# Gathering rows from a four-group loop with a ring of sixteen index columns, in a graph-network kernel

## The chip, the cores and the metric

One Trainium2 chip, one of its cores. The metric is the device time of one execution in microseconds (us), median of several runs. TensorE (PE) multiplies, VectorE (DVE), ScalarE (ACT) and GpSimd (POOL) work on tiles in on-chip memory, SyncE (SP) issues plain transfers. Only GpSimd issues indirect transfers here, the gathers of this case.

## The reference, cut to what matters

Four layers of message passing over one graph with 6250 nodes and 100000 edges, sorted by destination, features of 128 float32. Each layer reads a row of a node table for the source of every edge, combines it with something of the edge and of its destination, and reduces over the edges of one destination:

```
h1   = relu([x[src], edge_attr] @ W1a + b1a) @ W1b + b1b; segment_sum(h1, dst)     # layer 1
m    = xl[src] + xr[dst] + e_attr @ We;  logits = (leaky(m) * att).sum             # layer 2, twice
h3   = relu([x[dst], x[src] - x[dst]] @ W1 + b1) @ W2 + b2; segment_max(h3, dst)   # layer 3, three times
```

These are the six places where rows are gathered by `src`. Layer 0 (an attention layer) needs no such gather: it makes its rows by products and scatters sums instead.

## The kernel before

Edges are laid out in steps of 128, none of which crosses a block of 128 destinations. Four steps make a group (`GROUP = 4`), and every stage runs over 208 groups (`GROUPS`), the loops in trips of four groups (`RING = 4`, `trips = 52`), so that the buffer number `r = n % 4` is fixed in the code of a trip. `srci` holds the source numbers of all steps in on-chip memory, one column of 128 int32 for each step. One indirect transfer reads one column and brings 128 rows of the table from memory into a part of buffer `R[r]`, so a group takes four of them; each has a semaphore of its own, `rows_in[r][u]`.

The order between engines is kept by counting semaphores. A `Signal` starts with a lead of four, so `wait_ge(s, s.done(n - RING))` waits until group n-4 has been done, and lets the first four groups through.

**GpSimd before.** In `edge_mlp_sums` (line 987, layer 1), `edge_logits` (line 1198, twice in layer 2) and `edge_maxima` (line 1674, three times in layer 3) GpSimd's code has no loop: all 208 groups (209 in `edge_maxima`) are written out, each with a wait for its buffer and four transfers that name their column of `srci` directly. In `edge_mlp_sums` and `edge_maxima` the wait is part of the first of the four transfers. In `edge_logits` there are two waits: one on `products_made`, with a step `sem_inc(pool_gate)` of its own, and one on `rows_free_again`, which is part of the first transfer.

**What frees a buffer.** In `edge_mlp_sums` it is `rows_added`: DVE has added the gathered rows to PE's products (`join`, line 1058). In `edge_logits` it is `products_made` (PE, lines 1247 and 1249) and `rows_free_again`, which SP counts up (line 1210) once it has also stored the gathered rows to memory. In `edge_maxima` it is `edges_made`: PE has turned the rows (line 1713) and added the destinations' part (line 1717).

**The round of `edge_maxima`.** For every group PE runs `make_products(n)` (line 1723; waits for ACT's relu of group n), `make_edges(n + 1)` (1713, 1717), `turn(n - 1)` (1705) and `make_ends(n - 3)` (1730). ACT runs `lay(n + 2)` (1755), `relu(n + 1)` (1761; waits for `edges_made` of group n+1) and `turn_out(n - 1)` (1766). DVE runs the running maximum `scan(n)` (1802), `make_hots`, `add` (964) and `mark_ends`.

**ACT.** It does one relu per group in `edge_mlp_sums` (line 1043) and nothing in `edge_logits`.

**A stage that scatters.** `add_messages` in layer 0 is not changed, but it already has the form of the new code: GpSimd loops over 52 trips, waits at steps of its own (`sem_inc(pool_gate)`) and names columns of `slots`, a tile of sixteen columns, that DVE writes (line 835) before each group's four scatters (line 882).

Of the kernel before, what the change touches and what calls it, by code (L numbers as in the profile page):

```python
# [25 lines left out]
P = 128  # L26
# [94 lines left out]
def build(nc, I, out):  # L121
    ctx = ExitStack()
    with ctx:
# [843 lines left out]

        def edge_mlp_sums():
# [11 lines left out]
            with nc.Block() as block:  # L980
                @block.gpsimd
                def _(gp):
                    for n in range(GROUPS):
                        gp.wait_ge(rows_added.h, rows_added.done(n - RING))
                        for u in range(GROUP):
                            k = LEAD + n * GROUP + u
                            gp.indirect_dma_start(part(R[n % RING], u), None, gather_d[:, :],  # L987
                                                  bass.IndirectOffsetOnAxis(ap=srci[:, k:k + 1], axis=0)).then_inc(rows_in[n % RING][u].h, 16)
# [47 lines left out]
                @block.scalar  # L1036
                def _(act):
                    relued.lead(act)
                    with act.Fori(0, trips) as j:
                        for r in range(RING):  # L1040
                            n = j * RING + r
                            act.wait_ge(rows_added.h, rows_added.done(n))
                            S_.activation(M[r], M[r], ACT.Relu).then_inc(relued.h, 1)

                @block.vector
                def _(dve):
# [45 lines left out]
                    add(GROUPS - 1, RING - 1, ends)  # L1092
            for s in (edges_made, sums_made, relued, rows_added, hots_made, added):
                s.passed(GROUPS + RING)
# [80 lines left out]
        def edge_logits(heads, width, table, att, we):  # L1175
# [13 lines left out]
            with nc.Block() as block:  # L1189
                @block.gpsimd  # L1190
                def _(gp):
                    for n in range(GROUPS):
                        gp.wait_ge(products_made.h, products_made.done(n - RING))
                        gp.sem_inc(pool_gate.h, 1)
                        gp.wait_ge(rows_free_again.h, rows_free_again.done(n - RING))
                        for u in range(GROUP):
                            k = step_of(n) + u
                            gp.indirect_dma_start(part(R[n % RING], u, width), None, table[:, :],  # L1198
                                                  bass.IndirectOffsetOnAxis(ap=srci[:, k:k + 1], axis=0)).then_inc(rows_in[n % RING][u].h, 16)
# [53 lines left out]
                def _(dve):  # L1253
# [28 lines left out]
                    for r in range(RING):  # L1282
# [3 lines left out]
                        reduce(n, r)  # L1286
            for s in (products_made, logits_in, logits_made, rows_free_again):
                s.passed(GROUPS + RING)
# [5 lines left out]
            pool_gate.passed(GROUPS)  # L1294
# [360 lines left out]
        def edge_maxima(w2, next_weights):  # L1655
# [11 lines left out]
            with nc.Block() as block:  # L1667
                @block.gpsimd
                def _(gp):
                    for n in range(GROUPS + 1):  # L1670
                        gp.wait_ge(edges_made.h, edges_made.done(n - RING))
                        for u in range(GROUP):
                            k = LEAD + n * GROUP + u
                            gp.indirect_dma_start(part(R[n % RING], u), None, gather_d[:, :],  # L1674
                                                  bass.IndirectOffsetOnAxis(ap=srci[:, k:k + 1], axis=0)).then_inc(rows_in[n % RING][u].h, 16)
# [71 lines left out]
                def _(act):  # L1747
                    for s in (relued, laid):
                        s.lead(act)
                    turned_out.lead(act, 1)  # L1750

# [6 lines left out]
                    def relu(n, i):  # L1758
                        act.wait_ge(edges_made.h, edges_made.done(n))
                        act.wait_ge(products_made.h, products_made.done(n - 2))  # L1760
# [10 lines left out]
                    relu(0, 0)  # L1771
                    with act.Fori(0, trips) as j:
                        for r in range(RING):
# [4 lines left out]
                            relu(n + 1, 1 - r % 2)  # L1778
# [4 lines left out]
                def _(dve):  # L1783
# [53 lines left out]
                    add(GROUPS - 1, 1, ends[2 * GROUP:])  # L1837
            loaded.passed(16 * len(next_weights))
# [113 lines left out]
```

## Time and profile before

| | us |
|---|---|
| median of 3 runs | 11882.29 |
| lowest, highest | 11880.79, 11889.4 |
| span of the profiled execution | 11983.4 |
| GpSimd busy in that span | 6587.1 |
| PE / DVE / ACT busy | 7468.0 / 6860.6 / 2573.8 |
| mean granted TensorE clock | 0.773 |

The profiled execution is one execution under the profiler; its span is from the first to the last instruction, and no other time of that execution is given. Busy times of engines overlap. A stage's start and end are read from the first and last gather of its line: about 2273 to 3560 us (`edge_mlp_sums`), 3820 to 5095 and 6042 to 7325 (`edge_logits`), and three stretches between 8014 and 11940 (`edge_maxima`).

### The profile page before, as it was taken

How to read it: one execution, taken by the hardware profiler on the slowest of the kernel's cores; microseconds unless marked ns; L12 is line 12 of the kernel's file. 1: busy time of each engine (PE TensorE's matmuls, PEld its weight loads, DVE VectorE, ACT ScalarE, POOL GpSimd, SP SyncE). 2: the span in 40 equal slices, each digit the busy share in tenths (PEclk: the TensorE clock that was granted, in tenths of full speed). 3: DMA queues.
4: the chain of work that ended last, by engine and by line, in shares of the span. 5: the costliest groups of instructions: out<-in, count | busy, mean ns of one | idle time of the engine just before them, and what ended most of it. 6: DMA issues, size and time to landing. Idle time of an engine off the chain costs nothing. (4 is left out here: it accounts for less than half of the span.)

```text
span 11983.4 us, 181872 instructions
## 1 busy us (share of the span) xinstructions
PE 7468.0 (62%) x39289; PEld 6257.1 (52%) x39290; DVE 6860.6 (57%) x13795; ACT 2573.8 (21%) x9089; POOL 6587.1 (55%) x6703
## 2 busy tenths in 40 slices
PE   5944444366665777736565554667777676766676
PEld 4944444355555555524454444655555555555555
DVE  6845444433335888866644445665555555565555
ACT  3500000111111000036600001333333233323332
POOL 0088888466651666613256663326666566646665
PEclk8956666555557888879976666779999899989998
DMA  4355555322223666645444443423333333333333
GB/s 124 73 96 96 96 95 95 98 66 66 67 58 76 216 215 213 219 85 160 128 119 127 127 128 100 113 79 130 129 131 130 118 131 129 129 117 130 131 131 120
DMA packets 829515, 1435.73 MB, mean 120 GB/s; under 512 B 184832, under 2 KB 495468, under 8 KB 788960
## 3 DMA queue, kind: packets, MB, share of 16 engines
q1 hardware_dynamic: 532336, 981.36, 25.8%
q0 software_dynamic: 297072, 453.23, 17.4%
q14 instruction: 75, 0.61, 0.0%
q8 instruction: 32, 0.52, 0.0%
HBM read 1114.85 MB, written 320.07 MB: 120 GB/s over the span
## 5 line engine op out<-in xcount | busy, mean ns | idle before, releaser
L1674 POOL DMA_INDIRECT T<-gather_d,srci x2508 | 2386.0, 951 | 1655.8 <-remote 618.6
L1723 PE MATMUL PS<-T,W 128*128 128x512 f32 x1248 | 816.5, 741 | 1102.5 <-issue 601.4
L882 POOL DMA_INDIRECT added_d<-T,slots x832 | 1293.7, 1555 | 284.0 <-issue 215.6
L1249 PE MATMUL PS<-T,ident 128*128 128x256 f32 (+1 forms) x3328 | 1086.0, 410 | 544.6 <-issue 377.1
L964 DVE TENSOR_TENSOR T<-T,PS 128x128 f32 (+1 forms) x2098 | 561.0, 286 | 1267.7 <-remote 935.2
L1247 PE MATMUL PS<-T 128*128 x3328 | 1050.4, 400 | 347.5 <-issue 343.7
L1198 POOL DMA_INDIRECT T<-wide_d,srci x832 | 844.2, 1015 | 686.0 <-PEq L71 267.6
L987 POOL DMA_INDIRECT T<-gather_d,srci x832 | 822.2, 988 | 583.9 <-issue 232.9
L1249 PEld LDWEIGHTS PS<-T,ident 128*128 128x128 f32 x3328 | 717.7, 244 | 768.7 <-issue 463.9
L1198 POOL DMA_INDIRECT T<-gather_d,srci x832 | 800.4, 962 | 578.8 <-issue 234.5
L1469 PE MATMUL PS<-T 128*128 128x260 f32 (+1 forms) x3328 | 758.5, 384 | 445.8 <-DVEq L1522 392.7
L1263 DVE SCALAR_TENSOR_TENSOR T<-W,ew,PS 128x256 f32<-128x256 f32 (+1 forms) x1664 | 575.3, 408 | 775.6 <-remote 757.6
L1247 PEld LDWEIGHTS PS<-T 128*128 128x128 f32 x3328 | 733.5, 246 | 460.0 <-issue 403.3
L1448 POOL TENSOR_TENSOR T<-T,LG 128x256 f32<-128x256 f32 (+1 forms) x840 | 420.6, 522 | 1001.2 <-PE PS L1469 740.3
L1802 DVE TENSOR_TENSOR_SCAN T<-T,PS 128x512 f32<-128x512 f32 x624 | 796.2, 1276 | 243.6 <-issue 214.1
L1761 ACT ACTIVATE T<-PS 128x512 f32<-128x512 f32 x627 | 374.3, 597 | 2517.1 <-remote 1830.0
L1469 PEld LDWEIGHTS PS<-T 128*128 128x128 f32 x3328 | 594.7, 228 | 609.7 <-DVEq L1522 521.0
L800 PE MATMUL PS<-T 128*128 128x128 f32 x1664 | 421.1, 433 | 779.4 <-DVE T L839 779.4
L1723 PEld LDWEIGHTS PS<-T,W 128*128 128x128 f32 x1248 | 200.9, 202 | 1217.4 <-issue 887.4
L800 PEld LDWEIGHTS PS<-T 128*128 128x128 f32 x1664 | 360.3, 319 | 836.5 <-DVE T L839 836.5
L1717 PE MATMUL PS<-T 128*128 128x128 f32 x5016 | 760.4, 302 | 45.8 <-DVE T L1808 44.0
L1518 DVE TENSOR_TENSOR T<-T,PS 128x260 f32 (+1 forms) x1664 | 562.7, 354 | 381.6 <-issue 212.1
(254 smaller groups left out, 15227.1 us busy)
## 6 DMA issues: line engine op xcount, KB each, us to landing
T<-quads_d SPq DMA_DIRECT2D x315, 1024.0 KB
T<-edge_rows_d SPq DMA_DIRECT2D x210, 512.0 KB
edge_rows_d<-T SPq DMA_DIRECT2D x209, 512.0 KB
T<-onehot_t_d SPq DMA_DIRECT2D x416, 256.0 KB
T<-gather_d,srci POOLq DMA_INDIRECT x4172
T<-edge_rows_d SPq DMA_DIRECT2D x210, 256.0 KB
onehot_t_d<-T SPq DMA_DIRECT2D x208, 256.0 KB
edge_rows_d<-T SPq DMA_DIRECT2D x208, 256.0 KB
```

What stands on the lines that cost most here:

```text
L800: last = T_.matmul(part(bank(2 + i), u), part(EQ[i], u), part(MS[i], u), start=True, stop=True)
L882: gp.indirect_dma_start(added_d[u][:, :], bass.IndirectOffsetOnAxis(ap=slots[:, k:k + 1], axis=0), part(OUT[r], u), None, compute_op=ALU.a ...
L987: gp.indirect_dma_start(part(R[n % RING], u), None, gather_d[:, :], bass.IndirectOffsetOnAxis(ap=srci[:, k:k + 1], axis=0)).then_inc(rows_ ...
L1198: gp.indirect_dma_start(part(R[n % RING], u, width), None, table[:, :], bass.IndirectOffsetOnAxis(ap=srci[:, k:k + 1], axis=0)).then_inc(r ...
L1247: T_.matmul(spot(r, u), part(OT[r], u), T2[:, bass.ds(bs[i * GROUP + u] * width, width)], start=True, stop=False)
L1249: last = T_.matmul(spot(r, u), ident[:, :], part(R[r], u, width), start=False, stop=True)
L1263: last = V.scalar_tensor_tensor(part(M[r], u, width), we, ew[:, bass.ds(step_of(n) + u, 1)], spot(r, u), ALU.mult, ALU.add)
L1469: last = T_.matmul(spot(r, u), part(O[r], u), part(M[r], u, both), start=True, stop=True)
L1674: gp.indirect_dma_start(part(R[n % RING], u), None, gather_d[:, :], bass.IndirectOffsetOnAxis(ap=srci[:, k:k + 1], axis=0)).then_inc(rows_ ...
L1717: last = T_.matmul(part(edges, u), part(AB[r % 2], u), part(OT[r % 2], u), start=False, stop=u == GROUP - 1)
L1723: T_.matmul(bank(2 + i), w2, RT[i], start=True, stop=True).then_inc(products_made.h, 1)
L1802: V.tensor_tensor_scan(SC[i], firsts[r], bank(2 + i), SC[1 - i][:, GROUP * P - 1:GROUP * P], ALU.add, ALU.max).then_inc(scanned.h, 1)
```

## The change

In all six stages GpSimd's code becomes a loop of 52 trips over four groups, and its transfers read their columns from the ring `slots` (sixteen columns, four for each `r`). ACT copies the four columns of a group from `srci` into the ring (`take_numbers`). It copies the first four groups at the start; from then on, when the buffer of group n is free, it copies the columns of group n+4. GpSimd no longer waits for DVE or PE but for ACT's copy (`slots_made`), at a step of its own (`sem_inc(pool_gate)`). In `edge_logits` ACT, idle so far, gets a loop for it, and GpSimd's second wait (`rows_free_again`) is at a step of its own too. In `edge_mlp_sums` and `edge_maxima` the copy stands in front of the relu, behind the same wait.

```diff
+        def take_numbers(n, r):
+            S_.activation(slots[:, r * GROUP:(r + 1) * GROUP], srci[:, bass.ds(LEAD + n * GROUP, GROUP)], ACT.Copy).then_inc(slots_made.h, 1)
+        def gather_group(gp, table, rows, r, width):
+            gp.sem_inc(pool_gate.h, 1)
+            for u in range(GROUP):
+                k = r * GROUP + u
+                gp.indirect_dma_start(part(rows, u, width), None, table[:, :],
+                                      bass.IndirectOffsetOnAxis(ap=slots[:, k:k + 1], axis=0)).then_inc(rows_in[r][u].h, 16)
...
 # edge_mlp_sums, GpSimd
-                    for n in range(GROUPS):
-                        gp.wait_ge(rows_added.h, rows_added.done(n - RING))
-                        for u in range(GROUP):
-                            k = LEAD + n * GROUP + u
-                            gp.indirect_dma_start(part(R[n % RING], u), None, gather_d[:, :],
-                                                  bass.IndirectOffsetOnAxis(ap=srci[:, k:k + 1], axis=0)).then_inc(rows_in[n % RING][u].h, 16)
+                    with gp.Fori(0, trips) as j:
+                        for r in range(RING):
+                            gp.wait_ge(slots_made.h, slots_made.done(j * RING + r))
+                            gather_group(gp, gather_d, R[r], r, P)
 # edge_mlp_sums, ACT
+                    slots_made.lead(act)
+                    for r in range(RING):
+                        take_numbers(r, r)
                             act.wait_ge(rows_added.h, rows_added.done(n))
+                            take_numbers(n + RING, r)
                             S_.activation(M[r], M[r], ACT.Relu).then_inc(relued.h, 1)
...
 # edge_logits, GpSimd and ACT
-                    for n in range(GROUPS):
-                        gp.wait_ge(products_made.h, products_made.done(n - RING))
-                        gp.sem_inc(pool_gate.h, 1)
-                        gp.wait_ge(rows_free_again.h, rows_free_again.done(n - RING))
-                        for u in range(GROUP): ...
+                    with gp.Fori(0, trips) as j:
+                        for r in range(RING):
+                            n = j * RING + r
+                            gp.wait_ge(slots_made.h, slots_made.done(n))
+                            gp.sem_inc(pool_gate.h, 1)
+                            gp.wait_ge(rows_free_again.h, rows_free_again.done(n - RING))
+                            gather_group(gp, table, R[r], r, width)
+                @block.scalar
+                def _(act):
+                    slots_made.lead(act)
+                    for r in range(RING):
+                        take_numbers(r, r)
+                    with act.Fori(0, trips) as j:
+                        for r in range(RING):
+                            n = j * RING + r
+                            act.wait_ge(products_made.h, products_made.done(n))
+                            take_numbers(n + RING, r)
...
 # edge_maxima, GpSimd and ACT
-                    for n in range(GROUPS + 1):
-                        gp.wait_ge(edges_made.h, edges_made.done(n - RING))
-                        for u in range(GROUP): ...
+                    with gp.Fori(0, trips) as j:
+                        for r in range(RING):
+                            gp.wait_ge(slots_made.h, slots_made.done(j * RING + r))
+                            gather_group(gp, gather_d, R[r], r, P)
+                    gp.wait_ge(slots_made.h, slots_made.done(GROUPS))
+                    gather_group(gp, gather_d, R[0], 0, P)
-                    def relu(n, i):
+                    def relu(n, i, r):
                         act.wait_ge(edges_made.h, edges_made.done(n))
+                        take_numbers(n + RING, r)
                         act.wait_ge(products_made.h, products_made.done(n - 2))
                         S_.activation(RT[i], bank(i), ACT.Relu).then_inc(relued.h, 1)
```

## Rows read from the trace of the kernel before

**Rows 1.** Windows: a stage each; busy us and instructions by engine, clock, DMA.

```profile
2273.00:3560.00 1287.00, 837.32 (x3309) 738.33 (x3310) 446.07 (x1235) 131.03 (x207) 822.17 (x832) 0.50 0.24 66
3820.00:5095.00 1275.00, 929.95 (x3328) 700.00 (x3328) 1066.81 (x1446) 0.00 (x0) 844.23 (x832) 0.85 0.66 215
6042.00:7325.00 1283.00, 736.83 (x3328) 629.89 (x3328) 633.24 (x1451) 0.00 (x0) 800.41 (x832) 0.67 0.43 128
8014.00:9290.00 1276.00, 888.11 (x5432) 710.98 (x5432) 707.76 (x1466) 399.64 (x1257) 794.00 (x836) 0.91 0.39 130
```

**Rows 2.** Timeline, GpSimd, edge_maxima: start, duration, line, idle before.

```profile
8309.90 0.94 POOL L1674 DMA_INDIRECT T<-gather_d,srci  x1 [1.35 <-remote]
...
8313.65 0.95 POOL L1674 DMA_INDIRECT T<-gather_d,srci  x1 [0.30 <-issue]
```

**Rows 3.** Timeline, ACT, the same stretch: the relus of two groups.

```profile
8309.75 0.60 ACT L1761 ACTIVATE T<-PS 128x512 f32<-128x512 f32 x1 [3.81 <-remote]
...
8315.79 0.60 ACT L1761 ACTIVATE T<-PS 128x512 f32<-128x512 f32 x1 [4.17 <-remote]
```

**Rows 4.** Timeline, PE, the same stretch.

```profile
8310.40 1.12 PE L1723 MATMUL PS<-T,W 128*128 128x512 f32 x2 [2.18 <-issue]
...
8311.79 1.06 PE L1717 MATMUL PS<-T 128*128 128x128 f32 x8
```

**Rows 5.** Timeline, DVE, the same stretch: the scan.

```profile
8311.87 1.27 DVE L1802 TENSOR_TENSOR_SCAN T<-T,PS 128x512 f32<-128x512 f32 x1
```

**Rows 6.** Timeline, end of the first edge_maxima: GpSimd's last gather.

```profile
9274.51 0.94 POOL L1674 DMA_INDIRECT T<-gather_d,srci  x1 [0.30 <-issue]
```

**Rows 7.** Timeline, ACT, the same end.

```profile
9279.89 0.60 ACT L1761 ACTIVATE T<-PS 128x512 f32<-128x512 f32 x1 [1.34 <-PE PS L1717]
...
9283.41 0.60 ACT L1761 ACTIVATE T<-PS 128x512 f32<-128x512 f32 x1 [0.60 <-PE PS L1717]
```

**Rows 8.** Timeline, DVE and GpSimd, edge_mlp_sums.

```profile
2813.00 0.69 DVE L1058 TENSOR_TENSOR T<-PS,T 128x512 f32<-128x512 f32 x1 [9.64 <-remote]
...
2813.96 1.14 POOL L987 DMA_INDIRECT T<-gather_d,srci  x1 [3.15 <-DVE T L1058]
```

**Rows 9.** Timeline, DVE, add_messages, ahead of the first scatter.

```profile
580.69 0.16 DVE L835 TENSOR_TENSOR slots<-T,LG 128x4 int32<-128x4 f32 x1
```

**Rows 10.** Timeline, ACT and GpSimd, the same stretch.

```profile
580.05 0.60 ACT L863 ACTIVATE T<-PS 128x512 f32<-128x512 f32 x1 [11.55 <-PE PS L800]
```

```profile
581.65 1.80 POOL L882 DMA_INDIRECT added_d<-T,slots  x1 [12.66 <-DVE slots L835]
```

**Rows 11.** Groups by form, ACT: a copy of 128x4.

```profile
L1479 ACT ACTIVATE T<-LG 128x4 f32 x208 | 43.4, 209 | 289.4 <-PE PS L1469 287.4 <-PEq L71 2.0
```

**Rows 12.** Timeline, edge_maxima: eight gathers in one run, and the relu behind.

```profile
8784.75 0.95 POOL L1674 DMA_INDIRECT T<-gather_d,srci  x1 [0.30 <-issue]
```

```profile
8787.34 0.60 ACT L1761 ACTIVATE T<-PS 128x512 f32<-128x512 f32 x1 [3.12 <-remote]
```

**Rows 13.** Window of the slower clock; columns as in rows 1.

```profile
8316.80:8320.10 3.30, 3.30 (x12) 2.27 (x11) 2.48 (x4) 0.86 (x5) 2.39 (x4) 0.50 0.35 124
```

**Rows 14.** Timeline, second edge_logits: first and last gather of sixteen, DVE.

```profile
6601.03 0.94 POOL L1198 DMA_INDIRECT T<-gather_d,srci  x1 [4.80 <-SPq L1210]
...
6619.97 0.94 POOL L1198 DMA_INDIRECT T<-gather_d,srci  x1 [0.30 <-issue]
```

```profile
6624.06 1.12 DVE L1263 SCALAR_TENSOR_TENSOR T<-W,ew,PS 128x128 f32<-128x128 f32 x4 [11.62 <-remote]
```

**Rows 15.** Waits by stage: who, for what, us in total, times, longest.

```profile
POOL T L987 <- DVE T L1058: 224.5, 67, 5.8
```

```profile
POOL T L1198 <- SPq L1210: 160.1, 45, 5.1
```

```profile
POOL T L1198 <- SPq L1210: 212.9, 46, 5.4
```

**Rows 16.** Groups by form, GpSimd: the scatters of add_messages.

```profile
L882 POOL DMA_INDIRECT added_d<-T,slots x832 | 1293.7, 1555 | 284.0 <-issue 215.6 <-DMA added_d<-T,slots 55.8 <-DVE slots L835 12.7
```

More of the change, by code:

```diff
@@ L1092, in _ @@
                     add(GROUPS - 1, RING - 1, ends)
+            slots_made.passed(GROUPS + 2 * RING)
+            pool_gate.passed(GROUPS)
             for s in (edges_made, sums_made, relued, rows_added, hots_made, added):
@@ L1191, in _ @@
                 def _(gp):
-                    for n in range(GROUPS):
-                        gp.wait_ge(products_made.h, products_made.done(n - RING))
-                        gp.sem_inc(pool_gate.h, 1)
-                        gp.wait_ge(rows_free_again.h, rows_free_again.done(n - RING))
[L1196 to L1199, printed above, removed]
+                    with gp.Fori(0, trips) as j:
[15 more added lines that the diff above has]
+                            take_numbers(n + RING, r)
                 @block.sync
@@ L1286, in _ @@
                         reduce(n, r)
+            slots_made.passed(GROUPS + 2 * RING)
             for s in (products_made, logits_in, logits_made, rows_free_again):
@@ L1293, in edge_logits @@
                     rows_in[r][u].passed(16 * trips)
-            pool_gate.passed(GROUPS)
+            pool_gate.passed(2 * GROUPS)
             vv_done.passed(1)
@@ L1669, in _ @@
                 def _(gp):
-                    for n in range(GROUPS + 1):
-                        gp.wait_ge(edges_made.h, edges_made.done(n - RING))
[L1672 to L1675, printed above, removed]
+                    with gp.Fori(0, trips) as j:
[4 more added lines that the diff above has]
+                    gather_group(gp, gather_d, R[0], 0, P)
                 @block.sync
@@ L1750, in _ @@
                     turned_out.lead(act, 1)
+                    slots_made.lead(act)
+                    for r in range(RING):
+                        take_numbers(r, r)
                     def lay(n, i, bs):
@@ L1770, in _ @@
                     lay(1, 1, first[GROUP:])
-                    relu(0, 0)
+                    relu(0, 0, 0)
                     with act.Fori(0, trips) as j:
@@ L1777, in _ @@
                             lay(n + 2, r % 2, bs[r % 2 * GROUP:r % 2 * GROUP + GROUP])
-                            relu(n + 1, 1 - r % 2)
+                            relu(n + 1, 1 - r % 2, (r + 1) % RING)
                             turn_out(n - 1, 1 - r % 2)
@@ L1837, in _ @@
                     add(GROUPS - 1, 1, ends[2 * GROUP:])
+            slots_made.passed(GROUPS + 1 + 2 * RING)
+            pool_gate.passed(GROUPS + 1)
             loaded.passed(16 * len(next_weights))
```

## The prediction, as put on record before the run

> **What bounds the kernel now.** I read the windows of the stages first, then timelines inside a stage, then the waits. The windows [rows 1] show four stages of 208 groups that do very different work and yet take 1287, 1275, 1283 and 1276 us, so 6.13 to 6.19 us a group; the two later runs of `edge_maxima` have the same round. In none of them is any engine near full, except DVE in the first `edge_logits` (1066.8 of 1275). What they share is four gathers a group. A gather is 0.94 us with 0.30 between [rows 2], so four are 3.75 + 0.94 = 4.69 us, or 5.0 back to back: GpSimd is not full either, but it is nearest.
>
> The timeline of `edge_maxima` says how it paces. A round is 8315.79 - 8309.75 = 6.04 us [rows 3]. PE's L1717, which `edges_made` stands on, ends by 8312.85 [rows 4], yet ACT's relu, idle for 4.17 us, starts only at 8315.79 [rows 3]: 1.20 us after the last gather's end, 8313.65 + 0.94 = 8314.59 [rows 2]. GpSimd waits for the same signal. When no gather is left (the last ends at 9275.45 [rows 6]) the same round takes 9283.41 - 9279.89 = 3.52 us [rows 7]. So PE's results reach the other engines late while gathers run, and the loop is: release, restart of GpSimd (0.15 us after the relu's start: 8309.90 against 8309.75 [rows 2, 3]), 4.69 of gathers, 1.20 to the release. 0.15 + 4.69 + 1.20 = 6.04, the round. What delays PE's results is not visible; that it goes with the gathers is. Not every result is late: L1723 ends at 8311.52 [rows 4], 1.62 us after the run's first gather, and DVE's scan starts on it at 8311.87 [rows 5]; L1717 ends 2.95 after that gather and is late. Somewhere between the two the window closes.
>
> In the second `edge_logits` the same shows over sixteen gathers: they run 6601.03 to 6620.91, DVE resumes at 6624.06 after 11.62 idle, 3.15 behind them [rows 14].
>
> **The change part by part.** Four unrolled programs become loops. The branch costs nothing I can find: the scatters already run in such a loop, and all idle before 832 of them is 284.0 us, 0.34 each, the usual gap [rows 16]. GpSimd's steps between gathers run ahead of the transfers there, so I take them as 0; if that cover failed, 52 trips x 6 stages of a 0.3 us gap would be 94 us. The new column source: a scatter reads the same ring and its gap is as usual; a gather's 0.94 stays (0).
>
> The cost is the restart, where GpSimd has run dry. Three pieces.
> (a) ACT's copy: 128x4, 0.21 us [rows 11]. It starts where the relu starts now.
> (b) The step in front of the transfer. Where the wait is part of the transfer, DVE's join ends at 2813.69 and the gather starts at 2813.96 [rows 8]: 0.27. Where the wait is a step of its own, the ring is written by 580.85 [rows 9] and the scatter starts at 581.65 [rows 10]: 0.80; reckoned from ACT's end at 580.65 it is 1.00. I take 0.80; the other end is 0.27.
> (c) The relu itself comes later by the copy: 0.21 at most, some 0.1 if ACT overlaps them. It isn't on the loop in `edge_maxima` while PE's result lies 2.9 us waiting; in `edge_mlp_sums` PE's next wait is for DVE's additions. Queued behind the copy are the relu, then `turn_out` and `lay`; the nearest to need them is PE, with 2.18 us idle [rows 4]. I take 0; uncovered it would be 208 x 4 x 0.1 to 0.2, 83 to 175 us.
>
> `edge_maxima`: restart from the relu's old start is 0.21 + 0.80 = 1.01 against 0.15, so 0.86 more. If every group paid it: 3 x 208 x 0.86 = 537 us, the upper end. But GpSimd starting 0.86 later also lets PE get further before the window closes: L1717 then ends 2.95 - 0.86 + 0.11 = 2.20 after the first gather. That is between the delivered 1.62 and the late 2.95; I take it as delivered, since it is 0.58 from the one and 0.75 from the other, and keep the other answer as the upper end. Then the next group's gathers join the run with a gap of 0.30, and two groups share one restart. A run of eight exists: it ends at 8785.70 and the relu follows at 8787.34 [rows 12], 1.64 later. Cycle: 7 x 1.25 + 0.94 = 9.69, + 1.64 + 1.01 = 12.34, 6.17 a group. Of four rounds (24 us) one falls into a stretch at the clock 0.50, 1.2 GHz, which lasts 3.3 us or a little more [rows 13]; PE is slower there, L1717 comes too late, and the round is a single one, 6.04 + 0.86 = 6.90. Mean (3 x 6.17 + 6.90) / 4 = 6.35, 0.31 more, x 624 = **+195 us**. If runs grew to four groups: 19.88 [rows 14] + 3.15 + 1.01 = 24.04, 6.01 a group, -19 us: the lower end.
>
> `edge_mlp_sums`: GpSimd waits for DVE 67 times [rows 15]; each restart goes from 0.27 to 0.03 + 0.21 + 0.80 = 1.04: 67 x 0.77 = **+52**. Lower end 0 (67 x 0, if DVE's idle of 9.64 [rows 8] swallowed it).
>
> `edge_logits`: ACT's copy follows `products_made` and is done before SP has counted `rows_free_again`, which comes after SP's next store; its 0.21 is hidden. The second wait turns from part of the transfer into a step: 0.80 - 0.27 = 0.53 for 45 + 46 = 91 waits on SP [rows 15]: **+48**. Lower end 0, above all in the first, where DVE is 84% full [rows 1].
>
> Sum: 195 + 52 + 48 = 295. Against the span 11983.4 it gives 12278; the span is 101 us longer than the median of the runs, and I carry the difference over unchanged: 11882 + 295 = **12177 us**. This case's own ends: low -19 + 52 + 0 = +33, say 11,915 to 11,970; high 537 + 52 + 48 = 637, 12,519.
>
> **A page against it.** The loop above rests on gathers delaying PE's results. The Trainium skill ("SBUF — State Buffer", Who interferes with whom) states that a DMA never contends with a compute engine, apart from the port pair that GpSimd and DVE share. By that rule PE's 3.52 us round would not know of the gathers, GpSimd's later restart would drown in the three groups by which it runs ahead, and the time would stay near 11,882; by the rows it is 12,177. The rows [2, 3, 7] disagree with the rule as it stands, whatever the cause.
>
> **Rivals.**
> *Nothing (0.14).* GpSimd gathers group n+4 when group n is free, three rounds or 18 us ahead; a second later should not matter, if the common 6.04 to 6.19 us is set by something that goes on per gather whatever its start. For it: the equal times of unequal stages [rows 1]. Against: 0.15 + 4.69 + 1.20 gives the round [rows 2, 3]. Time 11,880 to 11,960; half of it within 0.2%.
> *Faster, the late results go away (0.11).* In all six stages a transfer with a wait inside lies in GpSimd's queue; in `add_messages`, whose waits are steps, GpSimd is busy with hardly a gap [rows 16] and PE's results reach ACT without such a delay [rows 10]. If the waiting transfer is the cause, the change removes it, and groups take 5.0 us (GpSimd), but DVE's 1066.8 in the first `edge_logits` [rows 1]: 3 x 208 x 1.04 = 649, then 1287 - 1040 = 247, 1275 - 1067 = 208 and 1283 - 1040 = 243: -1347, 10,535. Against: in `edge_maxima` the release follows the last gather's end [rows 2, 3], not the arrival of a wait.
> *Faster a little (0.09).* The later start lets so much of PE's work through that runs of three or four groups prevail and the round falls below 6.04 - (52 + 48 + 24)/624 = 5.84 us, from which it decides (100 us of the other two stages, 24 of the bound below): 11,750 to 11,850. Against: four-group runs by [rows 14] are 6.01.
> *Worse (0.04):* above 12,530, if the relu counts too.
>
> **How the numbers follow.** Likeliest 0.62. 0.2% of 11,882 is 24 us, about what a measurement tells from no change. Slower 0.62 + 0.04 + 0.06 = 0.72, same 0.08, faster 0.11 + 0.09 = 0.20. The range reaches down over the small gain and up to the upper end: 11,780 to 12,530; left out are the large gain, the worst case and some of the small gain, about 0.18. The likeliest case alone: 11,915 to 12,520.
>
> **What would show it.** In the new profile: the gathers at 0.94 us with gaps of 0.30, also across trips; in `edge_maxima` GpSimd's gap before a run 0.21 + 0.53 longer, 2.2 us or more where it was 1.35, and more often eight gathers in a run than four; the first relu of a run 1.2 to 1.6 us behind its last gather; windows of `edge_maxima` near 1320 us, of `edge_mlp_sums` near 1340, of the `edge_logits` 1300 to 1315. Wrong at its root if the relu no longer waits for the gathers' end, or if windows stay equal while GpSimd's gaps grow.

## The result, and the profile after

The changed kernel takes 12,204 us (12,202 to 12,212), the kernel before took 11,882 beside it: 1.0273 times as long, 95% interval 1.0261 to 1.0285, or 322 us more. Forecast were 12,177 and 295 more.

The stages of the changed kernel, each cut at its first gather's start and its last one's end (windows: start and end, length, busy time and instructions of PE, PE's loads, DVE, ACT, GpSimd, then clock, DMA share, GB/s); the third `edge_maxima` takes 1317:

```profile
2257.60:3578.80 1321.20, 832.43 (x3281) 732.15 (x3282) 453.32 (x1226) 149.37 (x410) 791.70 (x832) 0.50 0.24 64
3844.90:5130.50 1285.60, 923.35 (x3300) 689.54 (x3301) 1053.29 (x1427) 41.67 (x204) 863.82 (x832) 0.84 0.65 211
6097.10:7358.90 1261.80, 727.90 (x3314) 618.37 (x3314) 626.85 (x1433) 41.84 (x205) 806.75 (x832) 0.68 0.44 129
8058.80:9382.50 1323.70, 942.96 (x5340) 767.89 (x5341) 694.68 (x1438) 422.03 (x1444) 805.20 (x836) 0.83 0.38 124
9448.10:10766.10 1318.00, 943.15 (x5342) 768.89 (x5342) 685.53 (x1435) 424.75 (x1439) 803.14 (x836) 0.83 0.37 124
```

The windows of [rows 1] reach 7 to 15 us over the gathers. Cut at the gathers, as above, the stages of the first trace take 1280, 1263, 1273 and three times 1261 us (6.03 to 6.15 a group), and the six grew by only 230 us, the spans by 227 (12,210.1 and 11,983.4). The other 95 of the 322 are the profiled execution of before: it was 101 us longer than the runs that the median comes from. Its stages are as long as on a chip met further below (`three_ways`), where the kernel before takes 11,973 us and the unchanged first three stages take 1278, 1262 and 1271. The stages that an experiment left as they were show the usual pace. With the change in `edge_mlp_sums` alone, the windows of the two `edge_logits` and the first `edge_maxima` are:

```profile
3849.30:5097.30 1248.00, 920.12 (x3316) 692.62 (x3317) 1055.33 (x1430) 0.00 (x0) 841.08 (x832) 0.86 0.67 218
6057.90:7304.90 1247.00, 740.29 (x3318) 632.37 (x3318) 627.33 (x1435) 0.00 (x0) 801.16 (x832) 0.68 0.44 131
7999.10:9245.60 1246.50, 876.45 (x5342) 702.51 (x5342) 694.49 (x1438) 393.68 (x1237) 796.74 (x836) 0.90 0.40 132
```

and with it in `edge_maxima` alone, `edge_mlp_sums` is:

```profile
2272.30:3533.90 1261.60, 830.05 (x3280) 731.81 (x3280) 440.90 (x1223) 129.76 (x205) 825.80 (x832) 0.50 0.25 67
```

Against these the change costs 60 us in `edge_mlp_sums`, 38 + 15 in `edge_logits`, and 1323.7 + 1318.0 + 1317.2 - 3 x 1246.5 = 219 in `edge_maxima`: 332, where the timed runs have 322.

How `edge_maxima` runs now: the timeline of ACT, then of GpSimd, from one run of gathers into the next (start, duration, line, idle before; L970 is the copy of the columns, L1792 the relu, L977 the gathers).

```profile
8310.73 0.21 ACT L970 ACTIVATE slots<-srci 128x4 int32 x1 [3.12 <-remote]
8310.85 0.58 ACT L1792 ACTIVATE T<-PS 128x512 f32<-128x512 f32 x1
...
8315.44 0.20 ACT L970 ACTIVATE slots<-srci 128x4 int32 x1 [2.48 <-issue]
...
8323.33 0.20 ACT L970 ACTIVATE slots<-srci 128x4 int32 x1 [3.17 <-remote]
```

```profile
8311.72 0.94 POOL L977 DMA_INDIRECT T<-gather_d,slots  x1 [2.65 <-ACT slots L970]
8312.97 0.95 POOL L977 DMA_INDIRECT T<-gather_d,slots  x1 [0.30 <-issue]
...
8319.21 0.95 POOL L977 DMA_INDIRECT T<-gather_d,slots  x1 [0.30 <-issue]
8320.47 1.26 POOL L977 DMA_INDIRECT T<-gather_d,slots  x1 [0.30 <-issue]
...
8324.32 0.94 POOL L977 DMA_INDIRECT T<-gather_d,slots  x1 [2.59 <-ACT slots L970]
...
8328.06 0.95 POOL L977 DMA_INDIRECT T<-gather_d,slots  x1 [0.31 <-issue]
8329.85 0.94 POOL L977 DMA_INDIRECT T<-gather_d,slots  x1 [0.84 <-issue]
```

Eight gathers stand in a row where four stood [rows 2]. From the copy's start to the first gather it is 8311.72 - 8310.73 = 0.99 us, where the relu's start led the gather by 0.15. The run lasts 8321.73 - 8311.72 = 10.01, the copy follows 8323.33 - 8321.73 = 1.60 later, and the next run starts 0.99 behind it: 12.60 for two groups. Counted over the three stages, with a pause of 1.15 us or more as the end of a run, the trace holds 288 runs of eight (median cycle 12.63), 9 of seven, a few of other lengths and a single one of four, the last group of a stage. The relu isn't late by the copy: it starts 0.12 us behind the copy's start.

GpSimd's waits in the whole kernel (who, for what, us, times, longest), to be held against [rows 15]; the first row holds the waits at the starts of the stages too:

```profile
POOL T L977 <- ACT slots L970: 1937.5, 442, 266.1
POOL T L977 <- SPq L1236: 316.5, 81, 5.6
```

In `edge_mlp_sums` DVE's join, ACT's copy and GpSimd's restart follow each other like this:

```profile
2807.52 0.69 DVE L1072 TENSOR_TENSOR T<-PS,T 128x512 f32<-128x512 f32 x1 [7.21 <-remote]
```

```profile
2808.35 0.21 ACT L970 ACTIVATE slots<-srci 128x4 int32 x1 [8.64 <-DVE T L1072]
```

```profile
2809.34 0.95 POOL L977 DMA_INDIRECT T<-gather_d,slots  x1 [4.08 <-ACT slots L970]
```

From the join's end at 2808.21 to the gather it is 1.13 us, where it was 0.27 [rows 8].

### The profile page after: what moved, and what is told of

Same layout as the page of the kernel before. It is cut to its first block and busy times, and to the rows that moved or that the text cites. A ratio compares the mean times of both kernels' runs of the same rounds, so it can differ in the third digit from the quotient of the medians.

```text
span 12210.1 us, 188569 instructions
## 1 busy us (share of the span) xinstructions
PE 7674.8 (63%) x39289; PEld 6457.1 (53%) x39290; DVE 6843.4 (56%) x13795; ACT 2780.3 (23%) x10364; POOL 6608.8 (54%) x6703
## 5 line engine op out<-in xcount | busy, mean ns | idle before, releaser
L977 POOL DMA_INDIRECT T<-gather_d,slots x4172 | 4010.6, 961 | 3015.1 <-ACT slots L970 1665.3
L1750 PE MATMUL PS<-T,W 128*128 128x512 f32 x1248 | 859.2, 777 | 1054.4 <-ACT T L1792 1049.7
L970 ACT ACTIVATE slots<-srci 128x4 int32 (+1 forms) x1275 | 259.1, 205 | 5503.1 <-remote 2557.6
L977 POOL DMA_INDIRECT T<-wide_d,slots x832 | 863.9, 1038 | 687.9 <-ACT slots L970 272.1
L1833 DVE TENSOR_TENSOR_SCAN T<-T,PS 128x512 f32<-128x512 f32 x624 | 797.6, 1278 | 328.8 <-PE PS L1750 144.5
L1273 PEld LDWEIGHTS PS<-T 128*128 128x128 f32 x3328 | 728.1, 244 | 467.7 <-issue 413.4
L1496 PEld LDWEIGHTS PS<-T 128*128 128x128 f32 x3328 | 596.6, 229 | 609.2 <-DVEq L1549 520.0
L800 PE MATMUL PS<-T 128*128 128x128 f32 x1664 | 422.2, 434 | 780.4 <-DVE T L839 780.4
L1744 PE MATMUL PS<-T 128*128 128x128 f32 x5016 | 859.1, 328 | 64.9 <-DVE T L1839 33.9
L1744 PEld LDWEIGHTS PS<-T 128*128 128x128 f32 x5016 | 810.2, 245 | 73.9 <-issue 42.7
L800 PEld LDWEIGHTS PS<-T 128*128 128x128 f32 x1664 | 361.3, 320 | 836.9 <-DVE T L839 836.9
L1030 PE MATMUL PS<-T 128*128 128x129 f32 x1664 | 434.0, 442 | 474.4 <-ACT T L1057 343.7
```

The costliest lines, as they stand in the source:

```text
L800: last = T_.matmul(part(bank(2 + i), u), part(EQ[i], u), part(MS[i], u), start=True, stop=True)
L977: gp.indirect_dma_start(part(rows, u, width), None, table[:, :], bass.IndirectOffsetOnAxis(ap=slots[:, k:k + 1], axis=0)).then_inc(rows_in ...
L1273: T_.matmul(spot(r, u), part(OT[r], u), T2[:, bass.ds(bs[i * GROUP + u] * width, width)], start=True, stop=False)
L1496: last = T_.matmul(spot(r, u), part(O[r], u), part(M[r], u, both), start=True, stop=True)
L1744: last = T_.matmul(part(edges, u), part(AB[r % 2], u), part(OT[r % 2], u), start=False, stop=u == GROUP - 1)
L1750: T_.matmul(bank(2 + i), w2, RT[i], start=True, stop=True).then_inc(products_made.h, 1)
```

## The experiments

The runs went to several chips, and the kernel before, run beside each group, was not equally fast on them: 11,884 us beside the first four, 10,813 beside the next six, 11,973 beside `three_ways`, 11,879 beside `pauses`. Every ratio is against the kernel before on the same chip.

**The change in one stage at a time.** `maxima_only` and `mlp_only` are the kernel before with the changed function of that stage and the two helpers.

```diff
 # maxima_only: edge_maxima as changed; edge_mlp_sums, edge_logits as before
+        def take_numbers(n, r): ...
+        def gather_group(gp, table, rows, r, width): ...
-                    for n in range(GROUPS + 1):
+                    with gp.Fori(0, trips) as j:
 # mlp_only: the same in edge_mlp_sums alone
```

> The change in edge_maxima alone. The traces give its three runs 63 + 57 + 56 = 176 us of the 230 us by which the six stages grew, while the timed runs differ by 322. If the traces tell all of edge_maxima, the time is 11,882 + 176 = 12,058, and the missing 92 us lie in other stages. If those 92 us lie here, it is 12,150. If the three stages didn't cause it and something shared did (the ring, code loading at the start), it stays below 12,000.

> The change in edge_mlp_sums alone. By the traces +42 us (67 restarts of GpSimd, each 1.1 us longer, less some slow gathers): 11,924. If the missing 92 us of the timed runs lie here, 12,015. If a restart that GpSimd does while DVE waits for PE costs nothing: 11,882.

Measured: `maxima_only` 12,116 us, ratio 1.0217 (1.0177 to 1.0257; one of its six runs took 12,270), +232, between its forecasts of 12,058 and 12,150; `mlp_only` 11,925, 1.0035 (1.0022 to 1.0048), +42, as forecast. That leaves 322 - 232 - 42 = 48 us for `edge_logits`. The missing 92 us lay in no stage: the unchanged stages of both runs were shorter than those of the first trace.

**The step alone.** `own_step` is the kernel before but for

```diff
                         gp.wait_ge(edges_made.h, edges_made.done(n - RING))
+                        gp.sem_inc(pool_gate.h, 1)
                         for u in range(GROUP):
```

> The kernel before, with the wait of each group in edge_maxima at a step of its own; no copy, no ring, no loop. Theory A (the restart sets the round): GpSimd's idle before a run grows from 1.35 to 1.35 + 0.53 = 1.88 us. L1717 then ends 2.42 us after the first gather. If that is still late, every group pays: 3 x 209 x 0.53 = +332, 12,214. If it is delivered, runs of eight give 9.69 + 1.64 + 0.68 = 12.01 us for two groups and 6.57 for single ones; with one single in four rounds 6.15 a group, +67, 11,950. Theory B (only the copy ahead of the relu costs): no change. Theory C (GpSimd is three groups ahead, so its start doesn't matter): no change, and the idle before a run stays 1.35.

Measured: 12,006 us, 1.0099 (1.0085 to 1.0114), +122. B (only the copy costs) and C (GpSimd's start doesn't matter) fall. GpSimd's first gather follows the relu's start by 0.67 us (forecast 0.15 + 0.53), and the runs are of eight gathers. A's +67 was too low all the same: its cycle of 12.01 us measures 12.31 in the median. Timelines of ACT and GpSimd at a restart:

```profile
8315.16 0.60 ACT L1762 ACTIVATE T<-PS 128x512 f32<-128x512 f32 x1 [1.74 <-remote]
```

```profile
8315.83 0.94 POOL L1675 DMA_INDIRECT T<-gather_d,srci  x1 [2.61 <-remote]
```

**Loop and ring without the copy on the path.**

```diff
 # GpSimd, in the loop
                             gp.wait_ge(slots_made.h, slots_made.done(j * RING + r))
+                            gp.sem_inc(pool_gate.h, 1)
+                            gp.wait_ge(edges_made.h, edges_made.done(j * RING + r - RING))
                             gather_group(gp, gather_d, R[r], r, P)
 # ACT: the copy is made one group earlier, behind the relu
-                        take_numbers(n + RING, r)
...
+                            ahead(n + 2 + RING, j + (r + 2) // RING, (r + 2) % RING)   # waits for rows_in, then copies
```

> The loop and the ring in edge_maxima alone, but ACT copies a group's columns one group earlier and behind the relu, and GpSimd waits for edges_made itself, at a step of its own. Theory A: as own_step within 40 us, since both lengthen the restart by 0.53 and nothing else is on the loop; below maxima_only by 0.2 to 0.3 us for every restart, some 140 restarts x 3 x 0.25 = 105 us at most, or above it if fewer pairs of groups form. Theory D (the loop's code or the reading of the ring costs by itself): above own_step by more than 60 us, with gathers or the gaps inside a run longer than 0.94 and 0.30.

Measured: 12,059 us, 1.0148 (1.0133 to 1.0163), +175: 53 above `own_step`, between what A and D allow. Gathers (0.947 us) and the gaps in a run (0.31) are those of `own_step`, so neither the loop nor the ring is dear by itself. The runs of eight take 12.36 us against 12.31, and there are 78 rounds of four gathers, 6.5 us in the median, which `own_step` hardly has. Why the earlier copy makes these wasn't tried.

**Another order on PE.**

```diff
+                            make_edges(n + 1, j + (r + 1) // RING, (r + 1) % RING)
                             make_products(n, r % 2)
-                            make_edges(n + 1, j + (r + 1) // RING, (r + 1) % RING)
```

> The kernel before, with PE in edge_maxima doing make_edges(n + 1) ahead of make_products(n), which waits for relu(n). Theory A (results come out when a run of gathers ends, and early in it): edges_made is then made a round sooner, one release lets two groups through, and GpSimd runs eight gathers at a time: 9.69 + 1.87 = 11.56 us for two groups, 5.78 against 5.97, 627 x -0.19 = -119, about 11,765; longer runs would give more. Theory C (a fixed time for every gather sets the round): no change. A loss is possible if DVE's scan, which now waits longer for products_made, comes onto the loop: it would show as DVE's idle before the scan.

> The changed kernel with the same order on PE. Theory A: all runs are of eight gathers or longer, also in the stretches of the slower clock where now single rounds of 7 us stand. With eight: 9.69 + 2.84 = 12.53 for two groups, 6.27 against 6.32 now, -35, about 12,170; with sixteen: 19.7 + 3.9 = 23.6, 5.9 a group, -260, about 11,945. Rival: no change, since the changed kernel already lets a group's result through in the run.

> The kernel before with make_edges(n + 1) ahead of make_products(n), beside the same runs of the kernel before. Where the kernel before takes 11,880: theory A expects about -119, 11,765, and more if runs get longer than eight gathers; theory C no change. Where it takes 10,813: no change, as measured there already (ratio 1.0005).

Measured: `edges_first` 10,819 us, ratio 1.0005 (0.9996 to 1.0014); `edges_first_again` 10,816, 1.0004 (0.9994 to 1.0013); `edges_first_loop`, which holds the whole change, 10,806, 0.9995 (0.9986 to 1.0004). All three ran where the kernel before takes 10,813, and there GpSimd never waits for a buffer: the 832 gathers of each of the first three stages stand in one run. They say nothing for or against the order; the first run of `three_ways` does.

**The whole change on that chip.** The same changed kernel:

> The changed kernel once more. The kernel before took 11,882 us beside the first runs and 10,813 beside the last four, in which every stage's gathers ran back to back in one run of 832. Theory G (whether PE's results come late is a matter of the chip, and the change costs only where they do): where the kernel before takes 11,880, the changed one takes 12,204, ratio 1.027; where it takes 10,813, GpSimd never runs dry, no restart is paid, and the changed one takes 10,813 within 25 us, ratio 0.998 to 1.002. Theory H (the copies, steps and loops cost something on any chip): a ratio above 1.003 in both cases.

Measured: 10,803 us against 10,813, ratio 0.9989 (0.9980 to 0.9999): G holds, H falls. The first four gather stages, and then PE, ACT and GpSimd in the last of them:

```profile
2255.80:3313.10 1057.30, 847.24 (x3317) 740.29 (x3318) 457.12 (x1237) 150.83 (x414) 803.94 (x832) 0.50 0.30 81
3573.90:4680.40 1106.50, 833.04 (x3318) 615.00 (x3318) 1058.37 (x1440) 42.53 (x207) 853.33 (x832) 0.97 0.77 246
5632.60:6710.50 1077.90, 802.38 (x3318) 665.93 (x3318) 642.97 (x1447) 42.47 (x207) 824.65 (x832) 0.64 0.51 151
7403.00:8476.10 1073.10, 853.15 (x5373) 685.75 (x5373) 696.21 (x1451) 443.56 (x1456) 814.03 (x836) 0.93 0.46 153
```

```profile
7899.78 0.83 PE L1744 MATMUL PS<-T 128*128 128x128 f32 x6
```

```profile
7900.77 0.20 ACT L970 ACTIVATE slots<-srci 128x4 int32 x1 [1.67 <-PE PS L1744]
```

```profile
7900.57 0.95 POOL L977 DMA_INDIRECT T<-gather_d,slots  x1 [0.30 <-issue]
7901.82 0.94 POOL L977 DMA_INDIRECT T<-gather_d,slots  x1 [0.30 <-issue]
```

PE's result ends at 7900.61 and ACT starts on it at 7900.77, in the middle of a gather. GpSimd sets the pace, 5.08 to 5.32 us a group, and a copy or a step more is made three groups ahead of need.

**Fewer gathers, and rows by another way.**

```diff
 # three_gathers
-                        for u in range(GROUP):
+                        for u in range(GROUP - 1):
                             k = LEAD + n * GROUP + u
 # plain_rows: no GpSimd; SP, for each group
+                        sp.wait_ge(edges_made.h, edges_made.done(n - RING))
+                        for u in range(GROUP):
+                            k = (r * GROUP + u) * P
+                            sp.dma_start(part(R[r], u), gather_d[k:k + P, :]).then_inc(plain_in[r].h, 16)
```

> The kernel before with the fourth gather of every group of edge_maxima left out (a quarter of the rows are stale). Theory A: the round is restart and release, 1.27, and 3 x 1.25 - 0.30 = 3.44 of gathers: 4.71 us, 627 x -1.26 = -790, about 11,095. Theory C (a fixed time per gather, 5.97 / 4 = 1.49): 4.48 us, -934, about 10,950. If PE's or DVE's own work sets the round: no less than 5.97.

> The kernel before with no gathers in edge_maxima: SP brings as many rows of the same 512 bytes with plain transfers, four of 128 rows a group, from fixed places of the table (so the maxima are of wrong rows). Theory E (GpSimd's gathers delay PE's results): PE's results come out at once, as behind the last gather, and the round is near 3.52 us, or SP's four transfers if they take longer: 627 x -2.4 = -1500, about 10,380. Theory F (the rows' traffic into the chip's memory delays them): the round stays within 0.5 us of 5.97, and ACT's relu still starts 3 us behind PE's last matmul of L1717.

Both leave out part of the work, so their maxima are wrong: the first reads a quarter of its rows stale, the second reads the wrong rows. These too ran beside 10,813 us: 10,301 (ratio 0.9529) and 10,340 (0.9563), which tells what the stage takes without late results, not what makes them late. So one kernel with three forms of `edge_maxima` was made, in the order `edges_first`, `plain_rows`, `three_gathers`:

```diff
-                edge_maxima(at(n, 2), weights(n + 1) if n < 2 else [])
+                (edge_maxima_a, edge_maxima_b, edge_maxima_c)[n](at(n, 2), weights(n + 1) if n < 2 else [])
```

> The kernel before, with its three runs of edge_maxima made differently; edge_mlp_sums and edge_logits stay as they were and tell which of the two paces the execution has (6.0 us a group or 5.1). First run: PE does make_edges(n + 1) ahead of make_products(n). Second: the rows come by SP's plain transfers from fixed places of the table, not by GpSimd. Third: the fourth gather of every group is left out, so that a quarter of its rows are stale. Where PE's results come late: first run 1246 us without a gain (theory C), 1208 with runs of eight gathers (theory A: 5.78 a group), less with longer ones; second run 3.52 to 4.2 us a group, 740 to 880 us, if GpSimd's gathers delay the results (E), over 1100 us if the rows' traffic does (F); third run 4.71 us a group, 985 us, by restart and release (A), 4.48, 935 us, by a fixed time per gather (C). Where they don't come late: 1073, 740 to 880 and 895 us, as seen.

Measured beside 11,973 us: 11,355. Windows of `edge_mlp_sums` (unchanged) and of the three forms, the second from the first relu to the last:

```profile
2273.30:3551.20 1277.90, 829.96 (x3280) 731.88 (x3280) 441.74 (x1223) 129.76 (x205) 823.42 (x832) 0.50 0.24 66
8008.30:9270.30 1262.00, 893.26 (x5340) 701.70 (x5341) 683.56 (x1433) 402.77 (x1232) 814.04 (x836) 0.89 0.39 130
...
10317.10:11290.70 973.60, 780.11 (x5336) 631.60 (x5337) 707.13 (x1439) 391.82 (x1237) 591.91 (x627) 0.99 0.46 154
```

```profile
9365.20:10263.00 897.80, 760.98 (x5399) 626.83 (x5400) 666.54 (x1449) 424.49 (x1247) 0.00 (x0) 1.00 0.54 181
```

First, the order on PE gains nothing: 1262 us, as in the first trace of before, which has this chip's pace. Theory A's forecast of 1208 fails at "a round sooner", and at more than that: runs of eight gathers did become common (69, where each stage of the first trace has some ten), but such a pair takes 12.01 us in the median, where A had 11.56 and two single rounds take 12.08. PE's L1718 still waits in the middle of the group, here for ACT's `lay` (its row below; DVE's `make_hots` ends as late, at 8308.69):

```profile
8308.82 1.15 PE L1718 MATMUL PS<-T 128*128 128x128 f32 x8 [3.22 <-ACT T L1756]
```

By the code both `lay(n)` and `make_hots(n)` wait for `edges_made` of group n-2, so they too wait for the release, and `make_edges` with them. Second, without GpSimd's gathers the round falls to 4.3 us in the mean, with more bytes a second moved (181 against 130 GB/s), and ACT's relu starts 0.11 us behind PE's matmuls, which end at 9702.70:

```profile
9701.64 1.06 PE L1915 MATMUL PS<-T 128*128 128x128 f32 x8
```

```profile
9702.81 0.60 ACT L1959 ACTIVATE T<-PS 128x512 f32<-128x512 f32 x1 [0.60 <-PE PS L1915]
```

E holds and F falls, though 898 us is above the 740 to 880 expected. (The rows come from fixed places here, not scattered over the table, so the run tells GpSimd's gathers from the amount of traffic, not their issue from their scattered reads.) Third, with three gathers a round is 4.64 us. The timeline of ACT and GpSimd:

```profile
10804.87 0.60 ACT L2155 ACTIVATE T<-PS 128x512 f32<-128x512 f32 x1 [2.78 <-PE PS L2111]
...
10809.51 0.60 ACT L2155 ACTIVATE T<-PS 128x512 f32<-128x512 f32 x1 [2.48 <-PE PS L2111]
```

```profile
10805.03 0.94 POOL L2067 DMA_INDIRECT T<-gather_d,srci  x1 [1.21 <-PE PS L2111]
...
10807.52 0.95 POOL L2067 DMA_INDIRECT T<-gather_d,srci  x1 [0.30 <-issue]
10809.67 0.95 POOL L2067 DMA_INDIRECT T<-gather_d,srci  x1 [1.20 <-PE PS L2111]
```

Restart 0.16, gathers 3.44, release 10809.51 - 10808.47 = 1.04: 4.64. A expected 4.71, C (a fixed time for each gather) 4.48, both from the pace of 5.97. On this chip's 6.04, A gives 0.15 + 3.44 + 1.20 = 4.79 and C three quarters of it, 4.53. The measured round lies between, so this run doesn't decide for A. The stage takes 974 us, A 985, C 935.

**Pauses in GpSimd's work, and the change in `edge_logits`.**

```diff
 # edge_logits: as changed. edge_maxima, unrolled as before:
 # first run, behind gathers 0, 1, 2 of a group
+                            if u < GROUP - 1:
+                                gp.memset(rest[...], 0.0)     # 128x128
 # second run, behind gather 1; third run, ahead of gather 0
+                        gp.memset(rest[...], 0.0)             # 128x512
```

> edge_logits has the change, edge_mlp_sums is as before and tells the pace of the chip. The three runs of edge_maxima are as before but for work that only GpSimd does, on a tile of its own. First run: a memset of 128x128 behind each of the first three gathers of a group (0.19 us for such a one in the trace of before), so the gaps grow from 0.30 to 0.5 or more. Second run: one memset of 128x512 behind the second gather, a pause of 0.8 us or more in the middle. Third run: a memset of 128x512 in front of the first gather, behind the wait. Where PE's results come late: if they come out in such a pause, the rounds of the first two runs do not wait for the last gather's end and are what GpSimd's own work takes (5.6 to 6.2 us a group); if only the end of a run of gathers lets them out, they are the present round and the pauses, over 6.4 in the second and over 6.6 in the first. Third run: the later first gather acts as own_step did, more runs of eight gathers and 6.1 to 6.3 a group; no change if the wait's step itself, not the delay, made the cost. edge_logits: +48 us for its two runs (the 322 of the change less 232 and 42), 0 if the rest of the change's cost lies elsewhere. Where PE's results don't come late, every run is what GpSimd's work takes, near 5.1 and the pauses, and edge_logits has no difference.

Measured: 11,970 us beside 11,879, ratio 1.0077 (1.0060 to 1.0094). The windows of the two `edge_logits` and the three runs of `edge_maxima`:

```profile
3803.30:5085.60 1282.30, 930.46 (x3318) 695.65 (x3318) 1056.69 (x1433) 41.86 (x205) 860.88 (x832) 0.85 0.66 212
6045.50:7301.40 1255.90, 727.00 (x3318) 629.22 (x3318) 627.05 (x1433) 41.97 (x205) 806.87 (x832) 0.67 0.45 130
8002.40:9252.40 1250.00, 881.61 (x5342) 717.71 (x5343) 687.31 (x1438) 408.68 (x1238) 980.50 (x1463) 0.88 0.40 131
9317.60:10561.10 1243.50, 882.28 (x5342) 718.79 (x5342) 687.99 (x1438) 409.20 (x1237) 914.47 (x1045) 0.88 0.40 132
10626.20:11905.70 1279.50, 918.64 (x5342) 752.60 (x5342) 687.39 (x1438) 406.15 (x1237) 933.29 (x1044) 0.85 0.39 128
```

`edge_logits` costs 1282.3 - 1248.0 + 1255.9 - 1247.0 = 43 us, against `mlp_only`'s windows from another chip of the same pace; with the three runs of `edge_maxima`, 33 us together, the windows give 77 of the 92 us by which the timed runs differ. Timelines of GpSimd and ACT at a restart of the third run:

```profile
10919.58 0.53 POOL L2101 MEMSET rest<- 128x512 f32 x1 [1.19 <-remote]
...
10920.26 0.95 POOL L2104 DMA_INDIRECT T<-gather_d,srci  x1 [0.15 <-issue]
```

```profile
10919.63 0.60 ACT L2191 ACTIVATE T<-PS 128x512 f32<-128x512 f32 x1 [4.49 <-remote]
```

In the third run the memset starts with the relu (10,919.58 and 10,919.63) and the first gather at 10,920.26, 0.63 behind the relu, where `own_step` has 0.67. It costs 1279.5 - 1246.5 = 33 us a stage, `own_step` 1287.2 - 1246.5 = 41: it is the delay that costs, whatever makes it. The first two runs take 5.98 and 5.95 us a group. The pauses were shorter than expected: three gathers' starts lie 1.33 apart instead of 1.25 in the first, one 1.65 in the second, 0.25 and 0.40 more a group. A release that only the end of four gathers brings would give 5.96 + 0.25 = 6.21 and 6.36. So the pauses cost nothing, and they gain nothing either.

**What the release follows.** Counted from the last gather of a run, the release (ACT's start) comes at very different times, from 1.04 us behind three gathers to as much as 1.97 behind eight; DVE's comes 3.15 behind sixteen [rows 14]. Counted from the first gather, it hardly moves. In the medians it is 4.48 us behind the first of three gathers (`three_ways`), 5.80 behind the first of four (unchanged stage of `mlp_only`; 5.88 in the first trace), 11.64 for eight (`own_step` and the changed kernel; 11.74 in `mlp_only`), 17.56 for twelve (`mlp_only`) and 23.69 for sixteen (first form of `pauses`); [rows 14] have 6624.06 - 6601.03 = 23.03 for DVE. That is 1.44 to 1.49 for each gather, issued in 1.25. The runs of eight in `edge_maxima` of `own_step`, the changed kernel and `pauses`' third form tell the two ways of counting apart: they last from 9.7 to 10.6 us, because some of their gathers are slow or late, yet in about eight of ten the release lies 11.58 to 11.70 behind the first gather, and it doesn't grow with the length of the run. So the release isn't a fixed time behind the end of the gathers, as theory A and the prediction have it, but a fixed time for each gather reckoned from the restart: theory C's rate with theory A's restart. It explains why the pauses cost nothing, why pairs hardly gain (11.91 us in `mlp_only` against twice 5.96), and gives three gathers 0.16 + 3 x 1.47 = 4.57 of the measured 4.64. This was read from the traces afterwards; no run was made to try it, and what takes 1.45 us a gather isn't visible.

## Why the prediction was right

*The loop of `edge_maxima`* was right in that every round waits for a release which GpSimd's gathers hold back, and that a longer restart is paid in full. Lengthening the restart and taking GpSimd out moved the round as it says. Its release term was not: 1.20 behind the last gather, 1.64 behind eight, where the release stands at a fixed 1.45 us or so for each gather from the run's first. The restart, 1.01 by two rows of other stages, measures 0.99; its parts are the copy and the step, 0.53 forecast and 0.67 - 0.15 = 0.52 measured.

*Two groups share a restart*: right, but its reason was not, and two sizes were off and met, which is luck. I took L1717's result as delivered if it ends 2.20 us after the run's first gather, between 1.62 and 2.95. It doesn't end there. In the changed kernel PE starts on a release at 8311.56 and later at 8324.08, at a granted clock of 0.62 (8311.5 to 8315.5) and 0.50 (8324.0 to 8328.8):

```profile
8313.38 1.91 PE L1744 MATMUL PS<-T 128*128 128x128 f32 x8
...
8326.80 1.92 PE L1744 MATMUL PS<-T 128*128 128x128 f32 x8
```

The ends, 8315.29 and 8328.72, are 3.57 and 4.40 us into the run, and ACT's copies start 0.15 and 0.14 behind them (8315.44, and one at 8328.86). There is no early window that closes. Results come out at points inside a longer run as well, and what picks them isn't settled. The second size: I counted one single round of 6.90 in four, at the clock 0.50. There are none, because the later group of such a pair still joins, with a gap of 0.84 (8329.85 above). And a pair costs 12.63, not 12.34. The forecast took 9.69 for eight gathers and added the delay behind the last, 1.64. But the run that it read this from [rows 12] began at 8775.43 and lasted 10.27:

```profile
8775.43 0.94 POOL L1674 DMA_INDIRECT T<-gather_d,srci  x1 [1.39 <-remote]
```

Two groups need 11.64 from the first gather to the release, about twice the 5.80 of one group; with the restart of 0.99 that is 12.63. So pairing saves one restart and little else. With the forecast's own 12.34 and no single rounds it would have been (6.17 - 6.04) x 624 = +81 us. As it was, 6.32 a group came out where 6.35 was forecast, +219 to +232 us where +195 was; the 6.04 of the first trace is 5.96 in the runs that the median stands for.

*`edge_mlp_sums`*: 67 restarts at 0.77 were forecast, +52. The restart measures 1.13 against 0.27, 0.86 more, 58 us; the trace has +60, the timed run +42 (26 to 57). *`edge_logits`*: +48 forecast; 43 in the trace of `pauses`, 53 in that of the whole change, 48 by difference of the timed runs. *The loop's branch and the ring* cost nothing that can be seen: gaps across trips are 0.30, gathers 0.94. *The relu* is 0.12 later and not on the loop.

*The rivals.* "Nothing" and "a little faster" fall on the chips where results are late. "The late results go away" gives the right sort of time, 10,813 for its 10,535, but not by the change: the kernel before does it too on one chip, with its waits inside the transfers and its code unrolled. Of the page that was weighed (the Trainium skill, "SBUF — State Buffer", Who interferes with whom: a DMA never contends with a compute engine), the trace agrees on that chip (ACT 0.16 us behind PE in the middle of a gather). On the others results of a compute engine do come late while gathers run (2.94 us behind the end of PE's L1717 in [rows 3, 4]), but no run here shows whether that is contention for on-chip memory, which the page's rule is about.

The forecast carried the 101 us between span and median over as a constant. In the changed kernel's runs that difference is 6 us. It did no harm, since every term was a difference in restarts, and those hardly depend on the pace of the chip as long as results are late.

## What to carry to other kernels

Where an engine runs dry in every round, price a new link in its release chain by the restart, here a copy of 0.21 and a step of 0.5 us, times the number of restarts, and then ask how many groups will share one. Measure the rest of the cycle from the restart to the release as one piece, in runs of several lengths: twice the 5.80 us of a group and 0.99 for the restart give 12.59 for a pair, which takes 12.63, where gathers and a delay behind them gave 12.34. Where it never runs dry the same link costs nothing, so look first at the idle time before a run, not at the busy share. Compare kernels on one chip only, and if a profile's span and the median of the runs differ by a per cent, find an unchanged stage in another trace before reading differences of 1 or 2% stage by stage.

## What the runs showed of the hardware

One and the same kernel, the one before, took 10,813, 11,879, 11,884 and 11,973 us on the chips of this study. The difference is in how soon PE's results reach other engines while GpSimd issues gathers: at once on one chip, on the others often only when 1.44 to 1.49 us for each gather of a run have passed since its first began (4.48 us for three, 5.80 for four, 11.64 for eight). It showed with GpSimd's indirect gathers alone; SP's plain transfers of as many rows, from fixed places, didn't do it (0.11 us). What differs between the chips, and which results slip out inside a run, stays open. Two groups of runs met the chip with 10,813 us and both found it so; the others, as far as is recorded, were met once each. That it is the chip, and not something else that differs from one group of runs to the next, is likely but not shown.
